# Full attention: the value products of a step, cut into four quarters of 128 columns and set one behind each score product

## The reference, cut to what matters

```
q, k, v = proj(wq, bq), proj(wk, bk), proj(wv, bv)     # (B, 16, 1024, 8)
q, k = rotary(q), rotary(k)
scores = einsum('bhqd,bhkd->bhqk', q, k) * 8 ** -0.5
attn = softmax(scores, axis=-1)
out = einsum('bhqk,bhkd->bhqd', attn, v)
x = x + out.reshape(B, S, 128) @ wo.T + bo
```

## Time and profile before

| | us |
|---|---|
| median of 3 runs | 2496.29 (2495.68 to 2497.52) |
| profiled execution | 2495.79 |
| its span | 2494.0 |
| PE busy in it | 2176.5 (87%) |
| DVE busy | 1532.7 (61%) |
| ACT busy | 1188.0 (48%) |
| mean granted TensorE clock | 0.944 |

### The profile page before, as it was taken

One profiled execution on the slowest core, in us unless ns is written; L12 is line 12 of the kernel. 1 busy time (PEld: TensorE's weight loads), 2 busy tenths in 40 slices (PEclk: granted clock), 3 DMA queues, 4 the chain that ended last, 5 costly groups with the idle time before them and its releaser, 6 DMA issues. The chain is left out here.

```text
span 2494.0 us, 39867 instructions
## 1 busy us (share of the span) xinstructions
PE 2176.5 (87%) x15567; PEld 1185.3 (48%) x15567; DVE 1532.7 (61%) x2855; ACT 1188.0 (48%) x2084; POOL 376.8 (15%) x580
## 2 busy tenths in 40 slices
PE   5988997997988988998999999799669669995799
PEld 3665664664665664454222232244447554442345
DVE  7986986558986985116788888330586783038600
ACT  4764772355765772212477777632335533143221
POOL 4321331104322330002000000000114100000000
PEclk9999998998999999998799999999889889999799
DMA  3000000000000000002010100000001100000000
GB/s 137 4 6 3 4 6 7 2 13 38 4 7 2 4 6 28 0 0 71 20 31 21 31 21 21 10 0 0 5 1 36 54 1 9 0 1 0 0 0 17
DMA packets 39452, 38.80 MB, mean 16 GB/s; under 512 B 26882, under 2 KB 31618, under 8 KB 38498
## 3 DMA queue, kind: packets, MB, share of 16 engines
q1 hardware_dynamic: 38354, 34.90, 4.5%
q0 software_dynamic: 912, 1.35, 0.2%
HBM read 27.88 MB, written 4.46 MB: 13 GB/s over the span
## 5 line engine op out<-in xcount | busy, mean ns | idle before, releaser
L2250 DVE TENSOR_REDUCE fa_top<-psum 128x1 f32<-128x1024 f32 x256 | 305.2, 1221 | 76.9 <-PE psum L2193 75.9
L2239 ACT ACTIVATE fa_prob<-psum 128x512 f32<-128x512 f32 x512 | 278.9, 597 | 144.4 <-PE psum L2206 143.3
L549 DVE TENSOR_TENSOR scaled<-psum,area_b 128x512 f32<-128x512 f32 x16 | 11.1, 692 | 443.3 <-PE psum L518 443.3
L508 PE MATMUL psum<-hidden_b,area_b 128*128 128x512 f32 x512 | 221.7, 592 | 0.0
L508 PE MATMUL psum<-hidden_a,area_b 128*128 128x512 f32 x512 | 220.4, 592 | 0.0
L2193 PE MATMUL psum<-fa_stack_k,fa_stack_q 72*128 72x512 bf16 x512 | 204.4, 408 | 6.9 <-DMA fa_stack_k<-fa_ones 3.1
L2206 PE MATMUL psum<-fa_stack_q,fa_stack_k 74*128 74x512 bf16 x512 | 199.5, 393 | 10.0 <-ACT fa_prob L2239 4.4
L773 POOL TENSOR_TENSOR turn_a<-turn_a,turn_b 128x1024 f32<-128x1024 f32 x64 | 151.2, 2363 | 287.5 <-DVE turn_b L991 287.5
L790 PE MATMUL psum<-area_a,zt 128*128 128x512 f32 x256 | 136.0, 656 | 24.3 <-ACT k_t L922 14.3
L2206 PEld LDWEIGHTS psum<-fa_stack_q,fa_stack_k 74*128 74x128 bf16 x512 | 49.0, 97 | 225.8 <-ACT fa_prob L2239 196.3
L508 PEld LDWEIGHTS psum<-hidden_a,area_b 128*128 128x128 f32 x512 | 97.3, 190 | 122.5 <-issue 122.5
(11 more groups left out here) (365 smaller groups left out, 4290.1 us busy)
## 6 DMA issues: line engine op xcount, KB each, us to landing
area_b<-in_L_ffn SPq DMA_DIRECT2D x2, 2888.0 KB, 9.4
fa_stack_q<-fa_parts_dram SPq DMA_DIRECT2D x144, 32.0 KB
fa_stack_k<-fa_parts_dram SPq DMA_DIRECT2D x144, 32.0 KB
fa_parts_dram<-fa_prob SPq DMA_DIRECT2D x12, 256.0 KB, 2.5
area_a<-in_L_ffn SPq DMA_DIRECT2D x1, 2482.0 KB, 18.0
moved_halves<-y SPq DMA_DIRECT2D x16, 127.0 KB
area_b<-in_L_attn SPq DMA_DIRECT2D x1, 1880.5 KB, 20.0
area_a<-in_L_attn SPq DMA_DIRECT2D x1, 1538.0 KB, 6.4
```

Of the source, the lines that this page charges most:

```text
L508: last = nc.tensor.matmul(psum[:, 4 + n % 2, :], w(name)[:, k * TF_HID + m * P:k * TF_HID + (m + 1) * P], source[:, c, k, :], start=(k == ...
L2239: nc.scalar.activation(prob[:, (2 * s + j) % RING, half * CHUNK:(half + 1) * CHUNK], psum[:, 4 + n % 2, :], ACT.Exp, scale=float(D) ** -0. ...
L2250: nc.vector.tensor_reduce(top[:, g % 2, j, t:t + 1], psum[:, 2 * j:2 * j + 2, :].rearrange("p a n -> p (a n)"), AX.X, ALU.max, negate=True ...
```

## The change

The four value products of a step are cut into four quarters of 128 queries (`PER_CHUNK` is 4, `P` is 128). A quarter holds four products of 32 by 128 columns, one for each column tile. `pe_values` becomes a generator that gives one quarter at a time, and the loop takes one quarter behind each score and its `pe_max` product. The sum over the steps now begins with `start` in the first quarter of the first step alone. `used` is counted up behind the last quarter, so at the end of the step.

```
-            for j in range(2):
-                for half in range(2):
-                    at = GROUP * (2 * j + half)
-                    last = nc.tensor.matmul(psum[at:at + GROUP, 6 + g % 2, :], pair_v[:, g % 2, t, j, :],
-                                            prob[:, (2 * s + j) % RING, half * CHUNK:(half + 1) * CHUNK],
-                                            start=(t == 0), stop=(t == T - 1), tile_position=(0, at), skip_group_check=True)
-            last.then_inc(used.handle, 1)
+            for n in range(PER_CHUNK):
+                for j in range(2):
+                    for half in range(2):
+                        at, col = GROUP * (2 * j + half), half * CHUNK + n * P
+                        last = nc.tensor.matmul(psum[at:at + GROUP, 6 + g % 2, n * P:(n + 1) * P], pair_v[:, g % 2, t, j, :],
+                                                prob[:, (2 * s + j) % RING, col:col + P],
+                                                start=(t == 0 and n == 0), stop=(t == T - 1), tile_position=(0, at), skip_group_check=True)
+                if n == PER_CHUNK - 1:
+                    last.then_inc(used.handle, 1)
+                yield
...
                     ahead = pe_max(pe, s + AHEAD) if s + AHEAD < STEPS else iter(())
+                    values = pe_values(pe, s - LAG) if s >= LAG else iter(())
                     for j in range(2):
                         for half in range(2):
                             pe_score(pe, s, j, half)
                             next(ahead, None)
-                        if j == 0 and s >= LAG:
-                            pe_values(pe, s - LAG)
+                            next(values, None)
+                    for _ in values:
+                        pass
...
                 for s in range(STEPS - LAG, STEPS):
-                    pe_values(pe, s)
+                    for _ in pe_values(pe, s):
+                        pass
```

## The result

| | before | after |
|---|---|---|
| median, us | 2495.98 | 2758.42 (2755.94 to 2792.22, 4 runs) |
| ratio of the means (of the medians: 1.105) | | 1.109, 95% interval 1.100 to 1.117 |
| profiled execution, its span | 2495.79, 2494.0 | 2758.77, 2757.0 |
| mean granted TensorE clock | 0.944 | 0.857 |

The forecast was 2754 us, 4 us under the median. For the kernel with halves further down (e2), and for it alone, the ratio is taken over its faster executions, since its executions lie up to 88 us apart.

What follows compares the result with a forecast made beforehand. Neither ACT nor DVE set the pace; PE waited 0.24 us a step for ACT. Terms +14.1, +204.0, +23.1, +4.4, +11.7, +2.6, -1.7 gave +258: execution 2495.8 becomes 2754 us; own range 2735 to 2790, eight in ten 2546 to 2790.

Steps and rivals of the forecast that it cites:

- A quarter's price: Attention step: each quarter takes 0.36 us at the upper clock, including 0.24 for entering and leaving narrow tiles; step 3.56.
- The turn: Turn of the sums, once in 8 steps: costs 0.44 us in full at the upper clock, 0.85 at the lower.
- Steps 72 to 79: Steps in which the clock rises, at `pe_out` in step 78: 25.85 us become about 49, +23.1.
- The tail: Eleven steps without maximum products: 2.88 us becomes 2.7, winning 2.1 less 0.44 for one turn, -1.7.
- The clock: Largest term: PE stays at 1.2 GHz until `pe_out` in step 78, steps of 6.21 us, then stays up.
- Rival A: Clock rises as early as now because PE is kept continuously busy: +56, 2552 us; chance 17%.
- Rival B: A turn raises the clock in one of groups 1 to 8: from 2574 to 2730 us; chance 13%.
- The next `pe_out`: First `pe_out` fails to raise the clock, the next, 8 steps on, succeeds: +22, 2776 us; within the forecast's 55%.
- Rival D: Not slower: passages are hidden between small blocks, a step 2.6 us, 2440 us if the clock rises too; chance 7%.
- A sign that did not come: In the changed profile's attention stage, waits of scores for exponentials would be gone; no size given.
- The upper end: Attention step: 0.24 us of waiting per step is the most that spreading the value block can win.

Runs made afterwards that it cites:

- e2: Changed kernel with two halves of 256 columns in place of four quarters, from the first step on; ratio 1.013, executions of 2516.05 to 2603.65 us.
- e5: Changed kernel with wide value blocks in group 0 and two halves of 256 columns per step from the second group on; 2497.47 us, ratio 1.0003.
- e6: Changed kernel with a step's four quarters in one uninterrupted block at the old place, between the scores of head 0 and head 1; 2496.37 us, ratio 1.0013.
- e10: Kernel before, with halves in steps without maximum products and an unused float32 product in each of steps 1 to 10 ahead of the loop; 2486.14 us, ratio 0.9964.
- e1: Changed kernel with wide value blocks in group 0 (steps 2 to 9) and quarters from group 1 on; 2549.07 us, ratio 1.0215.
- e3: Changed kernel with 8 additional unused float32 products of 128 rows (16 passes) ahead of step 0; 2561.82 us, ratio 1.0257.
- e4: Changed kernel with 16 additional unused bfloat16 products of 72 rows ahead of step 0; 2770.3 us, ratio 1.109.
- e7: Changed kernel with 16 additional unused bfloat16 products of 128 rows ahead of step 0; 2552.6 us, ratio 1.0237.

## Why the prediction was right

Point by point, by the sum of the prediction, from the starts of the steps' first scores in the two traces:

| steps | predicted | measured |
|---|---|---|
| 2 to 7 | +14.1 | +14.1 |
| 8 to 71 | +204.0 | +204.9 |
| 72 to 79 | +23.1 | +25.3 |
| 80 to 87, 88 to 111, 112 to 116 | +4.4, +11.7, +2.6 | +4.8, +12.3, +2.8 |
| tail, to the turn behind the loop | -1.7 | -1.1 |
| sum | +258 | +263 (the spans differ by 263.0) |

The sum leaves out what lies outside the loop. There the two traces differ by -3.1 us ahead of step 0 and by +3.0 behind the last values; that these cancel is luck.

- **A quarter's price** was read from another stage's line of the same form, and held: 0.36 at the upper clock, 0.59 at the lower. The step is 3.58 for 3.56, which is 0.16 us in a group. e5 and e6 show that it is the passage: 0.24 for each block, 0.02 for the splitting. e10's float32 products leave no part of it to the change of type or rows.
- **The turn** was mis-sized: 0.50 us (1741.77 to 1742.27), not 0.44, and 0.91 at the lower clock (1265.43 to 1266.34), not 0.85. It stands behind narrow tiles now. With the step it makes the groups 29.14 instead of 28.92, and 50.64 instead of 50.5.
- **Steps 72 to 79** were 2.2 us too cheap. The sum took 1.5 off because the rise would fall into step 78; it came behind that step's `pe_out`, its last work, which took 1.87 us (1691.05 to 1692.92) and not 1.7.
- **The tail** was added up too well: 2.88 less 4 x 0.68 is 0.16, 1.8 us in eleven steps and not 2.1, so the same terms give -1.3.
- **The clock**, the largest term, stayed at 1.2 GHz until `pe_out` in step 78, as forecast. e1 and e3 show the cause in both directions: 8 wide blocks, or a run of 128-row products, and the quarters run at 2.4 GHz to the end. Rival A, the busy engine, falls with the changed kernel itself and with e4. The Trainium skill (TensorE: Matmul & The Clock Gate, section Why this matters for your kernels) advises keeping TensorE continuously busy to get the full clock. The traces disagree that this is enough: e4's has PE busy in every microsecond from 1253.58 to 1304.22, and its clock at 0.50 all the while.
- **Rival B**, a turn that raises the clock, did not come: four executions of 2756 us and more leave no room for it, since the latest such rise was priced at 2730. With halves it did (e2). The reason given against it, half a block, left out the piece that stands directly ahead of the turn. For quarters the two are 1.50 us and that made no difference; for halves they are 1.92 and it did.
- **The next `pe_out`**: one of four executions took 2792.22, 34 us more. I gave 22 us for a rise in step 86 instead of 78. It has no trace, but its mean granted clock is lower, 0.846 against 0.857 to 0.862. In e4's profiled execution, which took 2794.33 against a median of 2770.3, the rise stands behind the second `pe_out`, at 1759.8 us, and steps 72 to 87 took 22.7 us more than in the changed kernel's trace. So this is the likely reason there too; the other 11 of the 34 us stay open. That the first `pe_out` would suffice was a choice between two values, and it seems to have failed once in four executions.
- **Rival D**, hidden passages, falls with the quarter's 0.36 and with e5: 0.57 us for a half that streams in 0.43.
- **A sign that did not come**: the waits of scores for exponentials were to be gone and are still 101.6 us in the list, beneath the quarters. The steps of 3.58 and 6.2 show that they hold nothing up.
- **The upper end** for the gain was right: 0.24 us of waiting in a step was there to be won, and the first additional passage takes all of it.

## What to carry to other kernels

Before a block of matrix products is cut up to fill waits, price the passage between full-width products and column tiles, 0.24 us here, and pay it only where the wait is longer. Ask as well what raised the TensorE clock in the trace: if it was that block, cutting it can cost far more than the passages, and the place to look is the first stretch at 0.50 in which the engine is busy. A remedy that gave back some 200 us here (e3, e7) is to raise the clock ahead of the loop with a few microseconds of products on all 128 rows, even if nobody reads them.

## What was not expected

- PE can be busy without a gap for 500 us and stay at 1.2 GHz: from 1196 to 1693 us in the changed kernel, 44.14 of 44.14, then 50.64 of 50.64 in each of eight groups.
- A run of 16 bfloat16 products on 128 rows raised the clock, the same on 72 rows did not (4.2 us against 6.8 for the same number of columns).
- Cutting a float32 product into four narrower ones, with a weight load for each, costs 0.02 us in 1.00 (e6) as long as the pieces stay together.
- With halves the executions of one kernel differed by 88 us, 2516 to 2604. The one trace has the rise behind the fifth turn of the sums; the other times fit the fourth, second and first.
